# A convolution block on one core: four order tables of the same program, merged anew

## The reference

```
xc = conv2d(gn(x), conv1_w, conv1_b)          # 768 -> 16, 1x1
g = softmax(top-2 of (mean(xc) @ H_w.T + H_b)) # gates of 4 experts
for i in range(4):                             # experts
    up = resize(xc, 2**i); up = conv2d(up, convl_w); down = resize(up, 1)
out = x + conv2d(sum(down_i * g_i), conv2_w, conv2_b)   # 16 -> 768
```

## Time and profile before

| | |
|---|---|
| median of three runs | 1462.71 us (1459.87 to 1462.95) |
| profiled execution, its own time | 1463.79 us |
| its span, first to last instruction | 1462.1 us |
| TensorE, VectorE, ScalarE, GpSimd busy | 82%, 70%, 45%, 22% |
| moved by DMA | 540.01 MB, mean 369 GB/s |
| mean granted TensorE clock | 0.88 of 2.4 GHz |

### The profile page before, as it was taken

One profiled execution on the slowest core, in us unless ns is written; L12 is line 12 of the kernel. 1 busy time (PEld: TensorE's weight loads), 2 busy tenths in 40 slices (PEclk: granted clock), 3 DMA queues, 4 the chain that ended last, 5 costly groups with the idle time before them and its releaser, 6 DMA issues.

```text
span 1462.1 us, 24056 instructions
## 1 busy us (share of the span) xinstructions
PE 1206.2 (82%) x8700; PEld 818.7 (56%) x8700; DVE 1028.5 (70%) x2747; ACT 661.6 (45%) x1549; POOL 314.9 (22%) x381
## 2 busy tenths in 40 slices
PE   0789999989987899799887999888598998868752
PEld 0566677656755577466554766555365665535431
DVE  6889988688399788764688884669657845635843
ACT  2678998462523795644215864303251451100110
POOL 1082003403041000430440010254004105551000
PEclk9999999989978999799779999888796899887855
DMA  9798996699999999999999999999999999999998
GB/s 343 263 363 301 344 345 260 241 368 343 410 391 394 404 356 368 378 386 385 376 396 386 380 378 346 382 359 391 378 379 382 405 413 411 408 411 413 396 383 356
DMA packets 188162, 540.01 MB, mean 369 GB/s; under 512 B 12810, under 2 KB 12810, under 8 KB 188044
## 3 DMA queue, kind: packets, MB, share of 16 engines
q1 hardware_dynamic: 187772, 538.09, 96.4%
q10 hardware_dynamic: 272, 0.39, 0.1%
HBM read 337.12 MB, written 201.33 MB: 368 GB/s over the span
## 4 chain that ended last, share of the span: by engine, by line
PE 43%; DMA 28%; DVE 13%; ACT 6%; SPq 5%; issue 4%; POOL 1%; DVEq 0%; ACTq 0%; POOLq 0%
PE ring_ps L680 15%; DMA x_sb<-in_x 14%; DMA out<-x_sb 14%; PE conv_ps L750 10%; DVE x_sb L1004 9%; PE ring_ps L781 8%; PE img_ps L697 8%; SPq L512 3%; ACT xT L803 3%; DVE stats L920 2%; SPq L483 1%; PE ring_ps L769 1%; ACT unread_copy L827 1%; ACT unread_squares L825 1%; PE ring_ps L710 1%
## 5 line engine op out<-in xcount | busy, mean ns | idle before, releaser
L1004 DVE TENSOR_TENSOR x_sb<-x_sb,ring_ps 128x768 f32<-128x768 f32 x512 | 460.4, 948 | 312.0 <-PE ring_ps L781 186.3
L920 DVE BATCH_NORM_STATS2 stats<-x_sb 128x6 f32<-128x192 f32 x1792 | 473.0, 343 | 44.7 <-DMA x_sb<-in_x 39.4
L803 ACT COPY xT<-ring_ps 128x1024 f32<-128x1024 f32 x384 | 376.3, 1012 | 228.9 <-PE ring_ps L680 165.4
L680 PE MATMUL ring_ps<-ident,x_sb 128*128 128x128 f32 x3072 | 399.8, 283 | 66.8 <-DMA x_sb<-in_x 25.4
L680 PEld LDWEIGHTS ring_ps<-ident,x_sb 128*128 128x128 f32 x3072 | 348.7, 145 | 146.4 <-issue 89.4
L781 PE MATMUL ring_ps<-w,es 128*128 128x512 f32 (+1 forms) x1024 | 334.5, 443 | 111.7 <-DVE x_sb L1004 84.4
L781 PEld LDWEIGHTS ring_ps<-w,es 128*128 128x128 f32 x1024 | 188.5, 229 | 237.9 <-DVE x_sb L1004 148.6
L643 POOL TENSOR_TENSOR band<-taps,masks 128x640 f32<-128x640 f32 (+1 forms) x112 | 133.0, 1204 | 492.9 <-PE conv_ps L750 489.1
L750 PE MATMUL conv_ps<-xc,band 128*128 128x1 f32 (+8 forms) x1120 | 235.1, 360 | 4.0 <-issue 2.7
L697 PE MATMUL img_ps<-xT,w 128*32 128x256 f32 x3072 | 218.4, 393 | 16.9 <-ACT xT L803 13.2
L750 PEld LDWEIGHTS conv_ps<-xc,band 128*128 128x128 f32 x1120 | 168.0, 207 | 79.0 <-issue 76.2
(11 more groups left out here) (94 smaller groups left out, 343.8 us busy)
## 6 DMA issues: line engine op xcount, KB each, us to landing
x_sb<-in_x SPq DMA_DIRECT2D x128, 1536.0 KB, 11.4
out<-x_sb SPq DMA_DIRECT2D x256, 768.0 KB, 10.4
x_sb<-in_x SPq DMA_DIRECT2D x172, 768.0 KB, 9.5
w_rep<-in_L_conv_conv_w ACTq DMA_DIRECT2D x1, 384.0 KB
wl_raw<-in_L_conv_convl_w SPq DMA_DIRECT2D x8, 9.0 KB
gate_w<-in_L_conv_H_w SPq DMA_DIRECT2D x8, 0.2 KB
w_raw<-in_L_conv_conv_w SPq DMA_DIRECT2D x1, 48.0 KB
b_raw<-in_L_conv_conv_b SPq DMA_DIRECT2D x2, 3.0 KB
```

Source lines behind the costliest of these rows:

```text
L680: last = nc.tensor.transpose(ring_ps[:, buf, q, half * P:(half + 1) * P], slot("L", a, 2 * c + half)[:, q, k * P:(k + 1) * P], ident[:, :])
L803: nc.scalar.copy(xT[:, at % XT], ring_ps[:, TURN["T", a, n] % RING]).then_inc(xT_copied, 1)
L920: ins = nc.vector.bn_stats(stats[:, c, g, :], group)
L1004: nc.vector.tensor_tensor(x_sb[:, n, 2 * half + q % 2, :], x_sb[:, n, 2 * half + q % 2, :], flat_ps[:, TURN["E", b, t] % RING, 0:D], ALU.a ...
```

## The change

All four lists hold the same words in another order: the same 556 transfers with the same slots, and the same steps on TensorE, ScalarE and VectorE. Buffers, waits, code and `A_ORDER`, `B_ORDER`, `KEPT` are untouched. The lists get two lines longer in the file, so L680 of before is L682 of the changed kernel, and so on. One line of each list:

```diff
-L2.7:1 L1.0:5 L1.1:2 L1.2:3 L1.3:1 L1.4:7 S3.0.0 S3.0.1 S3.1.0 R3.2.0:4.0 S3.1.1 R3.2.1:4.1 R3.3.0:0.0 R3.3.1:0.1
+L2.7:1 L1.0:5 L1.1:2 L1.2:3 L1.3:1 L1.4:7 S3.0.0 S3.0.1 S3.1.0 R3.2.0:4.0 R3.2.1:4.1 S3.1.1 R3.3.0:0.0 L1.5:6 S3.2.0
...
-V T12.0-3 Z12 T12.4 M12.0-4 T12.5-8 M12.5 T12.9-10 M12.6-8 T12.11-12 M12.9-10 T12.13 M12.11-12 T12.14-17 M12.13-14
+V T12.0 Z12 T12.1-5 M12.0-3 T12.6 M12.4 T12.7 M12.5-7 T12.8-13 M12.8-11 T12.14 M12.12-13 T12.15 M12.14 T12.16-18
```

More of the change, by code:

```diff
@@ L60 @@
[L60 to L69, removed]
@@ new lines @@
+S5.0.1 L6.6:2 R5.1.1:6.1 L6.7:4 S5.1.0 L10.0:3 R5.2.0:6.0 S5.1.1 L10.1:11 R5.2.1:6.1 S5.2.0 L10.2:8 L10.3:9 L10.4:2
+R5.3.0:6.0 L10.5:4 S5.2.1 L10.6:10 R5.3.1:6.1 S5.3.0 L10.7:12 R5.4.0:6.0 S5.3.1 L11.0:0 R5.4.1:6.1 L11.1:5 S5.4.0
+S5.4.1 R5.5.0:6.0 R5.5.1:6.1 R5.6.0:12.0 R5.6.1:12.1 S5.5.0 S5.5.1 S5.6.0 R5.7.0:6.0 R5.7.1:6.1 L11.2:1 S5.6.1
+R6.1.0:12.0 S5.7.0 S5.7.1 R6.1.1:12.1 R6.2.0:6.0 R6.2.1:6.1 S6.0.0 S6.0.1 S6.1.0 R6.3.0:7.0 R6.3.1:7.1 R6.4.0:12.0
+S6.1.1 S6.2.0 S6.2.1 S6.3.0 R6.4.1:12.1 R6.5.0:6.0 R6.5.1:6.1 R6.6.0:7.0 S6.3.1 S6.4.0 S6.4.1 S6.5.0 R6.6.1:7.1
@@ new lines @@
+T15.18 M15.15-16 T15.19 E8.9 T15.20 E8.10 M15.17-18 E8.11 M15.19 E8.12 T15.21 E8.13 T15.22 M15.20 T15.23 X8.2 E8.14
+M15.21-23 E8.15 X8.3 G3 E8.16-17 H3 E8.18-28 C14.0 E8.29 C14.1-2 E8.30 C14.3-6 E8.31 X14.0-1 E14.0-8 C13.0 E14.9-11
+C13.1-2 E14.12-13 C13.3-4 X14.2 C13.5-6 E14.14-15 X14.3 E14.16-20 C15.0 E14.21-29 C15.1-4 E14.30-31 X13.0-1 E13.0-2
+C15.5-6 E13.3-13 X13.2 E13.14-15 X13.3 E13.16-24 C12.0-1 E13.25-31 X15.0-1 E15.0-10 C12.2-6 E15.11-13 X15.2 E15.14-15
+X15.3 E15.16-31 X12.0-1 E12.0-13 X12.2 E12.14-15 X12.3 E12.16-31
@@ new lines @@
+S9.0.28 D13 T13.2 S9.0.29 T13.3-5 S9.0.30 T13.6-7 S9.0.31 T13.8-9 S9.1.28-30 T13.10-11 S9.1.31 T13.12-13 S9.2.28
+T13.14-15 S9.2.29-30 T13.16 S9.2.31 T13.17 S9.3.28 T13.18 S9.3.29 T13.19-20 S9.3.30 T13.21 S9.3.31 T13.22-23
+S5.0.28-29 D9 I13 T9.0-2 S5.0.30 T9.3 S5.0.31 T9.4-6 S5.1.28 T9.7 S5.1.29-30 T9.8-10 S5.1.31 S5.2.28 T9.11-14 S5.2.29
+T9.15-16 S5.2.30-31 T9.17 S5.3.28 T9.18-21 S5.3.29-31 T9.22-23 I9 D5 T5.0-23 S7.0.28-29 I5 S7.0.30 P1 S7.0.31
+S7.1.28-31 S7.2.28-29 T7.0 S7.2.30 X0.2 S7.2.31 X0.3 S7.3.28-31 T7.1 D7 T7.2 H4 S14.0.28 T7.3-4 X4.0-1 T7.5-14
@@ new lines @@
+S14.0.29 T7.15-16 X4.2 T7.17-18 X4.3 T7.19-23 S14.0.30 I7 H7 X7.0 S14.0.31 X7.1-3 S14.1.28-31 S14.2.28 T14.0
+S14.2.29-31 S14.3.28-31 H5 X5.0 D14 X5.1 T14.1-4 S6.0.28 T14.5 S6.0.29-31 T14.6-8 S6.1.28 T14.9 S6.1.29 T14.10-16
+S6.1.30-31 T14.17 S6.2.28 T14.18 S6.2.29-30 T14.19 S6.2.31 S6.3.28-29 T14.20-21 S6.3.30 T14.22-23 S6.3.31 I14 T6.0 D6
+T6.1-8 S10.0.28 T6.9 S10.0.29-30 T6.10-11 S10.0.31 T6.12-16 X5.2 T6.17-23 S10.1.28 I6 S10.1.29-30 X5.3 S10.1.31
+S10.2.28-29 T10.0 S10.2.30-31 S10.3.28-31 S11.0.28 D10 T10.1-2 H6 T10.3-5 S11.0.29-31 T10.6-16 X6.0-1 T10.17-23 I10
@@ new lines @@
+P0 G0 B2.1.0-27 B2.2.0-27 B2.3.0-27 F2 B1.0.0-27 L3 A3.0-7 B1.1.0-27 A3.8-13 B1.2.0-20 A3.14 B1.2.21-27 A3.15-19
+B1.3.0-20 A3.20-21 B1.3.21-27 A3.22-26 F1 A3.27-31 L2 A2.0-28 B13.0.0-6 A2.29 B13.0.7-20 L1 A2.30-31 A1.0-10
+B13.0.21-27 B13.1.0-6 A1.11-13 B13.1.7-13 A1.14-21 B13.1.14-20 A1.22-26 B13.1.21-27 A1.27 B13.2.0-6 A1.28-29
+B13.2.7-27 A1.30-31 L0 B13.3.0-27 A0.0-1 F13 B9.0.0-27 B9.1.0-27 B9.2.0-27 B9.3.0-27 F9 B5.0.0-27 B5.1.0-27 B5.2.0-27
+B5.3.0-27 F5 B7.0.0-27 B7.1.0-27 A0.2-9 B7.2.0-20 A0.10 B7.2.21-27 A0.11-13 P1 G1 A0.14-15 B7.3.0-13 A0.16-19
@@ L195 @@
+A10.29 B11.3.7-13 A10.30-31 B11.3.14-27 A9.0-2 F11 A9.3-9 B15.0.0-27 B15.1.0-27 A9.10-25 B15.2.0-13 L11 A9.26-31
+B15.2.14-27 A11.0-11 B15.3.0-6 A11.12-14 B15.3.7-27 A11.15-19 F15 A11.20-24 L8 A11.25-31 A8.0-16 P3 A8.17 G3 A8.18-30
+L14 A8.31 A14.0-18 L13 A14.19-31 A13.0-21 L15 A13.22-31 A15.0-22 L12 A15.23-31 A12.0-31
 """
```

206 lines of the change are left out of this document (95 added, 111 removed).

## The result

The changed kernel takes 1476.21 us, the median of five runs (1473.90 to 1482.88), beside 1462.95 us of the kernel before, also five (1459.87 to 1470.76): a ratio of 1.0091, 95% interval [1.0055, 1.0126]. It is 0.9% slower, where 0.3% faster was forecast, and outside the range given. The profiled execution took 1473.90 us, with a span of 1472.2 us. The ratios leave out runs in a slower state, of which there were two in all, among the twelve of experiment 15, whose median still counts them.

A forecast was written before the change was run, and what follows sets the result against it. Compute engines, TensorE foremost, were taken to bound 84 to 300 us, then the DMA queue's depth. Terms 0 - 4 - 3 + 4 - 2 = -5 us gave 1458.8 from 1463.79, so 1458 us against the median; range 1449 to 1471.

The forecast's parts named there:

- What bounds the kernel: Compute engines set the pace from 84 to 300 us; afterwards the DMA queue, often shallow between 500 and 1100 us.
- The first 84 us: nothing: Start of the run: earlier moments of sample 12 change nothing; 0 us, bounds -1 and +1.
- Earlier moments: -4 us: 84 to 300 us: five moments earlier in TensorE's list cut VectorE's fold waits by 7.1 us; -4, bounds -8.4 and +2.
- The sum: Whole run: the terms 0 - 4 - 3 + 4 - 2 = -5 us.
- early moments hold TensorE: Rival, 84 to 300 us: each moment waits for statistics, +2 us in place of -4, about 1464 us; chance 0.07.
- The hole: -3 us: 280 to 340 us: sample 1's statistics fill VectorE's 7.03 us wait in sample 3; -3 us, bounds -5.7 and +1.
- the prediction had as its sign: Sign for the filled hole: more than 291 GB/s at 320 to 340 us.
- Refills: +4, bounds -12.5 and +12.9: 300 to 1360 us: more refills close behind their store cost 12.9 us, partly given back by shorter waits for additions; +4.
- The prices of the earlier trace: 300 to 1360 us: a refill costs 2.1 us with one half strip after its store, 0.9 us with two.
- 500 to 1100 us was where it should show: Sign for refills: under 370 GB/s there favours the slower rival, over 383 the large gain; before, 377.
- The end: -2 us: From 1360 us: one more half strip behind the last refill covers its landing; -2 us, bounds 0 and -7.8.

The follow-up runs named there:

- experiment 15: The kernel of experiment 9 with 32 more refills (up to three half strips in between) moved behind the next store: 1461.47 us, 0.9965 of before.
- experiment 4: The kernel before with the changed TensorE, ScalarE and VectorE lists up to the fold of sample 2 (about 255 us): 1476.72 us, 1.0075 of before.
- experiment 18: The kernel before with only the moments of samples 0, 4, 8, 3 and 2 earlier in TensorE's list, timed a second time: 1.0052 of before.
- experiment 7: The kernel before with 22 refills that had three half strips after their store moved one store ahead: 1491.79 us, 1.0199 of before.
- experiment 9: The kernel of experiment 3 with 19 refills with two or fewer half strips in between moved behind the next store: 1452.89 us, 0.9913 of before.
- experiment 16: The changed kernel, early part kept, with the 19 refill moves of experiment 9: 1458.37 us, 0.9964 of before.
- experiment 8: The kernel before with 18 refills with two or fewer half strips in between moved behind the next store: 1460.35 us, 0.9974 of before.
- experiment 3: The changed kernel with the engines' lists of before up to the first part B (about 255 us): 1471.16 us, 1.0043 of before.
- experiment 10: The kernel before with the changed order only from the last addition and store of sample 9 on (about 1000 us): 1468.42 us, 1.0018 of before.
- experiment 11: The kernel before with only sample 1's second statistics part moved behind 8 additions of sample 3 instead of 16: 1467.53 us, 1.0013 of before.
- experiment 2: The changed kernel with only SyncE's transfer list put back to that of before: 1497.72 us, 1.0233 of before.

## Why the prediction was wrong

**What bounds the kernel.** This reading held. From 84 to 300 us TensorE sets the pace: experiments 4 and 18 turned 10.2 and 5.5 us more of its idle time into 11 and 7.6 us. After that the order of refills and stores does (experiments 7, 9 and 16).

**The first 84 us: nothing.** No experiment took this part by itself; the first two of the 40 slices, of some 37 us each, are 343 and 261 GB/s, against 343 and 263.

**Earlier moments: -4 us. This is the step that failed.** All five alone gave +10 and +7.6 us, not -4, and outside the bounds of -8.4 and +2. In the changed kernel TensorE's idle time rose to 16.3 us, where it was to fall below 8.4, and VectorE's five waits fell only from 11.5 to 9.1 us in sum, not by 7.1. The sum took VectorE's wait for its first operand as what could go. Two things were missing. A fold has a second input, from ScalarE, whose list in experiment 18 still has it at its old place: 3.2 us of waiting became 15.6. And a moment takes one of the three PSUM buffers and holds TensorE until the statistics are there, so that transposes start later. In the changed kernel ScalarE's list was moved too, and the second wait is 4.0 us in all; there the cost is TensorE's, 4.57 us at once, and then 1.7 us by a stretch at half clock. The rival "early moments hold TensorE" named the mechanism, with 0.4 us for each and a time of 1464. One of them alone was eleven times that.

On the half clock the Trainium skill has a rule ("TensorE: Matmul & The Clock Gate", "Part 1: The HAM clock gate"): an array that has idled runs at half rate until it has been busy again. The trace agrees, with a granted clock of 0.50 from 94 to 98 us; I had counted idle time at its own length only.

**The gates.** The sum had no term for them. Alone they cost +4 us (1.0026): TensorE's idle time from 84 to 300 us is 9.4 us and not 8.4, and in the changed kernel 3.18 us of waiting stand at their new place. A step that moves by a few places on a full engine should have had its row.

**The hole: -3 us.** Right in that the wait went away, wrong as a gain: alone +0.1% with an interval that excludes -0.2%. That the queue loses 5.7 us at 320 to 340 us was true, but the additions were not what it lost them by: without the hole the rate there is 301 GB/s. That the changed kernel has 374 there, over the 291 that the prediction had as its sign, is no support for the step.

**Refills: +4, bounds -12.5 and +12.9.** This term was not measured by itself. What is left of the changed kernel without its early part is +0.43% (6 us), but that holds the hole, the refills and the end, for which the sum had -3 + 4 - 2 = -1. Less the late part (2.6 us) and the hole (1.9 us), each with an interval of some 3 us to either side, 1.5 us stay: within the bounds, and no closer than that. The prices of the earlier trace rows were about right where the depth was changed alone: 29 of 34.5 us in experiment 7, and 19 of 24.9 us in experiment 9. How much comes back was right in kind and wrong as a fixed share: about a sixth and a quarter there, and more than four fifths in experiment 8, against the two thirds that I had assumed. The Trainium skill ("DMA: Bandwidth & Descriptors", "Bandwidth") gives a longer transfer a higher rate, 341 GB/s for 1 MB and 425 for 16 MB, and my estimate from it was 0.8 us for a refill with two in flight. Experiment 9 agrees, with 19 us for 25 refills, and experiment 8, with 4 us for 25, does not. I was also wrong in that 500 to 1100 us was where it should show (381 GB/s, not below 377); the rate fell to 376 before it and to 393 behind it, where the earlier trace rows have 385 and 407.

**The end: -2 us.** Not seen: the late part alone gave 1.0018, and from 1360 us the rate rose to 392 GB/s only over a stretch that is 10 us longer.

**The sum.** The forecast had -4 us for the early part and -1 for the rest. Measured are +7 (experiment 3, or +11 by experiment 4) and +6. They are off by 11 and 7, together the 18 us that the forecast was off by. In the early part the gates make up to 4 of the 11 and the moments the rest; the parts taken alone (+4, and +7.6 to +10) come to more than +7, and intervals of 3 to 5 us to either side of each leave no finer split. In the rest, the hole and the end, forecast at -5 together, measured about +4.5 (experiments 10 and 11), and that carries the 7.

**What stays open.** Why 18 moves of refills bring 4 us on the list of before, and 19 such moves 19 us on the changed one. The rates tell where: with the 18 moves, 500 to 1100 us has 383 GB/s and not 377, but 1100 to 1360 us, whose transfers they leave in their places, has 398 and not 407; with the 19, 388 and not 377, and 401 and not 397. In the changed kernel additions are waited for less (114.9 us against 142.5), so a store that moves ahead costs less; this is argued and not shown.

## What to carry to other kernels

Where one engine sets the pace, price an order by the idle time that it gives to that engine, not by the waits that it takes from others: follow every input of the step that is to start earlier, on all engines, before its gain is counted. In one in-order queue, put more between a store and the refill that waits for it. Moving a refill with two half strips or fewer in between behind the next store was worth about 1 us on this order, but only 0.2 us on that of before, and only up to a point: 19 moves brought 1.3%, 32 more took 0.5% back. The waits of the queue didn't tell that point. Count all refills that a swap touches: each moves the store of another one too. Lists that were merged together can't be tested one at a time, but they can be cut by time.

## What the runs showed of the hardware

After one gap of 4.57 us TensorE ran at half clock from 94 to 98 us, 29 matmuls in place of 45: the price of a stall there is more than its length. At the same place, behind gaps of 3.36, 4.51 and 5.18 us, experiments 2, 16 and 4 have a clock of 0.50 from 93 to 94 us too, but means of 0.71, 0.74 and 0.88 from 94 to 98 us, so the length of the slow stretch did not go with that of the gap. In experiment 18, whose gaps around there are 1.19 us at most, the clock stayed at 1.00. A queue whose DMA share is 1.00 moved 377 GB/s or 388, by nothing but the place of 19 transfers in its list (500 to 1100 us in experiments 3 and 9): a share of 1.00 doesn't say that the DMA engines have no more to give.
